# A hand-ordered Strassen kernel for AdaLN and FFN with LoRA experts: in the second pair VectorE makes two rests earlier and ranks experts later, and in the third pair GpSimd makes one rest ahead of a sum

## The reference

```python
y = einsum('bct,bcd->bdt', x, weights[condition])      # 64x64 per sample, chosen by index
result = einsum('bnd,od->bno', y, W_base) + b_base      # 1024 -> 1024
logits = einsum('bnd,ed->bne', y, W_gate)               # 8 experts
top_p, top_i = top_k(softmax(logits), 2)                # renormalised to sum 1
route_w = sum(one_hot(top_i, 8) * top_p[..., None], axis=-2)
hw = einsum('bnd,erd->bner', y, A) * route_w[..., None] # rank 16 each, 128 columns in all
delta = einsum('bner,eor->bno', hw, B)
out = x + result + delta                                # the scaling is 16/16 = 1
```

## Time and profile before

| | |
|---|---|
| median of 3 runs | 938.79 us |
| lowest and highest | 938.47 and 940.17 us |
| the profiled execution | 938.57 us, of which the span in the trace is 936.8 us |
| TensorE busy | 930.6 us, 99% of the span |
| TensorE weight loads | 877.6 us (beside the matmuls) |
| VectorE busy | 661.9 us, 71% |
| GpSimd busy | 529.3 us, 56% |
| ScalarE busy | 383.1 us, 41% |
| granted TensorE clock | 1.0 in the whole run's mean |

### The profile page before, as it was taken

How to read it: one execution, slowest core, us unless ns; L and a number is a source line. 1 busy time by engine, 2 the same in 40 slices (tenths; PEclk the granted TensorE clock), 3 DMA queues, 4 the chain that set the end, 5 groups by cost and what they waited for, 6 DMA issues and landing times.

```text
span 936.8 us, 17713 instructions
## 1 busy us (share of the span) xinstructions
PE 930.6 (99%) x5402; PEld 877.6 (94%) x5402; DVE 661.9 (71%) x2281; ACT 383.1 (41%) x817; POOL 529.3 (56%) x514
## 2 busy tenths in 40 slices
PE   9999999999999999999999999999999999999998
PEld 7989999999999999999999999999999999999998
DVE  5887667676677676676766767667767667676675
ACT  6743343443434434434334344343443443433432
POOL 2896555654556545566555565455664556655550
PEclk9999999999999999999999999999999999999999
DMA  9423333323333233232233332333323423223312
GB/s 316 170 72 131 124 112 112 107 83 123 121 103 123 78 112 134 91 132 90 101 123 112 112 103 87 123 121 103 123 82 108 134 95 129 90 100 123 112 68 90
DMA packets 41484, 107.13 MB, mean 114 GB/s; under 512 B 4481, under 2 KB 8706, under 8 KB 41474
## 3 DMA queue, kind: packets, MB, share of 16 engines
q1 hardware_dynamic: 40930, 106.47, 32.7%
q10 hardware_dynamic: 544, 0.54, 0.2%
HBM read 73.43 MB, written 33.55 MB: 114 GB/s over the span
## 4 chain that ended last, share of the span: by engine, by line
PE 98%; POOL 1%; DMA 0%; DVE 0%; issue 0%; ACT 0%; POOLq 0%; DVEq 0%
PE ps L875 56%; PE ps_r L875 19%; PE ps_out L893 11%; PE ps_out L903 9%; PE ps L934 1%; PE ps L945 1%; PE ps_r L934 1%; DMA r_raw<-in_w_t 0%; POOL s_sum L333 0%; POOL a_lo L322 0%; POOL raw L352 0%; PE ps_r L920 0%; PE ps L920 0%; POOL s_sum L339 0%; POOL s_sum L347 0%
## 5 line engine op out<-in xcount | busy, mean ns | idle before, releaser
L322 POOL TENSOR_TENSOR a_lo<-raw,a_hi 128x512 fp32r<-128x512 f32 x128 | 167.2, 1318 | 139.5 <-ACT a_hi L434 137.4
L678 DVE STREAM_TRANSPOSE ps_hwt<-hw 32x32 f32<-32x32 f32 x944 | 210.3, 223 | 29.6
L875 PE MATMUL ps<-w_hi,s_hi 128*128 128x448 f32 x492 | 180.7, 367 | 1.3 <-issue 0.8
L875 PE MATMUL ps<-w_lo,s_hi 128*128 128x448 f32 x492 | 178.5, 363 | 0.0
L875 PE MATMUL ps<-w_hi,s_lo 128*128 128x448 f32 x492 | 178.2, 362 | 0.0
L875 PE MATMUL ps_r<-r_lo,a_hi 128*128 128x264 f32 x488 | 139.0, 285 | 0.0
L875 PE MATMUL ps_r<-r_hi,a_hi 128*128 128x264 f32 x488 | 138.6, 284 | 0.0
L875 PE MATMUL ps_r<-r_hi,a_lo 128*128 128x264 f32 x488 | 138.5, 284 | 0.0
L875 PE MATMUL ps<-w_hi,a_hi 128*128 128x448 f32 x376 | 137.2, 365 | 0.0
L875 PE MATMUL ps<-w_hi,a_lo 128*128 128x448 f32 x376 | 136.9, 364 | 0.0
L875 PE MATMUL ps<-w_lo,a_hi 128*128 128x448 f32 x376 | 136.5, 363 | 0.0
(11 more groups left out here) (146 smaller groups left out, 1683.2 us busy)
## 6 DMA issues: line engine op xcount, KB each, us to landing
raw<-in_x_t SPq DMA_DIRECT2D x128, 256.0 KB, 2.6
o_sb<-in_x SPq DMA_DIRECT2D x64, 512.0 KB, 3.6
out_x<-o_sb SPq DMA_DIRECT2D x62, 512.0 KB, 2.7
w_sum<-in_w_t SPq DMA_DIRECT2D x6, 448.0 KB, 9.1
w_sum<-in_w_t SPq DMA_DIRECT2D x4, 224.0 KB, 5.5
r_raw<-in_w_t ACTq DMA_DIRECT2D x2, 264.0 KB, 4.6
r_raw<-in_w_t SPq DMA_DIRECT2D x2, 264.0 KB, 6.1
table_raw<-in_cond_w SPq DMA_DIRECT2D x2, 256.0 KB, 8.1
```

Source lines behind the costliest of these rows:

```text
L322: pool.tensor_tensor(a_lo[j][:], raw[j][:], as_f32(a_hi[j][:]), ALU.subtract).then_inc(s_a_lo[j], 1)
L678: dve.transpose(ps_hwt[c * TURN:(c + 1) * TURN, r * TURN:(r + 1) * TURN], hw[r * TURN:(r + 1) * TURN, c * TURN:(c + 1) * TURN]).then_inc(s ...
L875: mm = pe.matmul(bank[:, 0:w.shape[-1]], a[:, k, :], w[:, k, :], start=(opens and k == 0 and q == 0), stop=(closes and k == KH - 1 and q = ...
```

## The change

It moves instructions and adds or removes none.

- **DVE, second pair.** The gate of tile a (`rank_experts(1, 0)`, `weigh_experts(1, 0)`) stood ahead of T1's and T3's rests and now stands behind both and behind `u2`. `hwt_rest(2)` moves behind T4's rest. `u3` comes ahead of the sum that adds P3, and the three outputs of tile a move behind the sums of P5 and P4.
- **PE, second pair.** `turn_hw(2)` moves from the half of P6 to the half of P7. Lora L and R of tile a move from ahead of P4 to behind it.
- **ACT, second pair.** T3's top and three tops of the third pair's input come ahead of the gate's exponential. The seeds and S3's top move back.
- **POOL, third pair's preparation.** S2's rest stands ahead of S3's sum.

SP's list is the same.

```diff
@@ POOL, first()
                 sum_s4(2)
+                s_rest(2, 2, s2[:], s2_hi, s2_lo)
                 sum_s3(2)
-                s_rest(2, 2, s2[:], s2_hi, s2_lo)
                 s_rest(2, 3, s3[:], s3_hi, s3_lo)
@@ ACT, first()
                 z_top(1, R, ps_5[:, 0:width[R]])
-                exps(2)
                 t_top(3, T3)
-                pe_hwt_top(3)
                 a_top(2, A11)
                 act.wait_ge(s_p[3], 2)
                 a_top(2, A12)
                 a_top(2, A21)
+                exps(2)
+                pe_hwt_top(3)
                 added_top(1, 0, Q, ps_r[:, 0:NS])
-                seed(1, 1, L)
                 added_top(1, 1, Q)
                 sum_top(2, 2, s2[:], s2_hi)
                 added_top(1, 1, L)
-                sum_top(2, 3, s3[:], s3_hi)
+                seed(1, 1, L)
                 seed(1, 1, R)
                 sum_top(2, 1, s1[:], s1_hi)
                 act.wait_ge(s_p[4], 2)
                 a_top(2, A22)
                 seed(1, 1, Q)
+                sum_top(2, 3, s3[:], s3_hi)
@@ DVE, first()
                 z_rest(1, 0, R, ps_r[:, 0:width[R]])
-                rank_experts(1, 0)
-                weigh_experts(1, 0)
                 z_rest(1, 1, R, ps_5[:, 0:width[R]])
                 t_rest(1, T1)
-                hwt_rest(2)
                 t_rest(3, T3)
                 dve.wait_ge(s_p1_out, 1)
                 dve.wait_ge(s_p[6], 2)
                 add(ps_6, p1, u2).then_inc(s_u2, 1)
+                rank_experts(1, 0)
+                weigh_experts(1, 0)
                 t_rest(4, NT4)
+                hwt_rest(2)
+                dve.wait_ge(s_p[7], 2)
+                add(ps_6, p1, u3).then_inc(s_u3, 1)
                 dve.wait_ge(s_p[3], 2)
                 dve.wait_ge(s_u2, 1)
                 add(ps_1, u2, u2).then_inc(s_p3_in, 1)
-                dve.wait_ge(s_p[7], 2)
-                add(ps_6, p1, u3).then_inc(s_u3, 1)
@@ PE, first()
-                strassen(ps_6, s2_hi, s2_lo, T2, True, lambda: turn_hw(2)).then_inc(s_p[6], 1)
+                strassen(ps_6, s2_hi, s2_lo, T2, True).then_inc(s_p[6], 1)
...
-                strassen(ps_6, s3_hi, s3_lo, T3, False).then_inc(s_p[7], 1)
+                strassen(ps_6, s3_hi, s3_lo, T3, False, lambda: turn_hw(2)).then_inc(s_p[7], 1)
                 mix_chunk(1, 0, R)
+                pe.wait_ge(s_t_lo[4], 1)
+                pe.wait_ge(s_u3, 1)
+                strassen(ps_6, a_hi[A22], a_lo[A22], NT4, False).then_inc(s_p[4], 1)
                 pe.wait_ge(s_hwt_lo, 3)
                 lora(0, L)
                 lora(0, R)
-                pe.wait_ge(s_t_lo[4], 1)
-                pe.wait_ge(s_u3, 1)
-                strassen(ps_6, a_hi[A22], a_lo[A22], NT4, False).then_inc(s_p[4], 1)
```

More of the change, by code:

```diff
@@ L794, in first @@
                 add(ps_5, u2, ps_r[:, 0:NS]).then_inc(s_z_sum[0, Q], 1)
-                output(1, 0, L)
                 added_rest(1, 0, Q, ps_r[:, 0:NS])
@@ L798, in first @@
                 add(ps_5, u3, u3).then_inc(s_z_sum[1, Q], 1)
-                output(1, 0, R)
                 added_rest(1, 1, Q)
@@ L802, in first @@
                 add(ps_6, p1, added[1, L]).then_inc(s_z_sum[1, L], 1)
+                output(1, 0, L)
                 added_rest(1, 1, L)
+                output(1, 0, R)
                 output(1, 0, Q)
```

## The result

| | before | after |
|---|---|---|
| median | 938.70 us (13 runs) | 940.46 us (13 runs) |
| lowest and highest | 938.46 and 940.28 | 939.90 and 943.23 |
| the profiled execution | 938.57 (span 936.8) | 941.5 (span 939.8) |

The ratio is 1.0023, with a 95% interval of 1.0015 to 1.0031: the change makes the kernel **slower by 0.2%**, just over the bound up to which I had called a difference none. The ratio is worked out from all executions; the two medians alone are 1.76 us, or 0.19%, apart.

What follows compares the result with a forecast made beforehand. PE, busy for 99% of the span, was taken to bound the kernel, so only its waits count. New waits of 2.69 less old ones of 2.32 gave +0.37 us and 939.1 us, with a range of 937.9 to 940.7.

Steps and rivals of the forecast that it cites:

- What bounds the kernel: PE busy for 99% of the span; the change moves only its waits in that stretch, 2.3 us at most to win.
- my second case: Rival of two port turns lost: the sum of S2 goes ahead of T4's rest, P4 at 63.08; +1.45, 940.2 us, chance 0.30.
- The exclusive port: A DVE operation with both inputs in SBUF and a POOL operation don't run together; the later waits for the whole earlier one.
- T4's rest, issued "at 59.10": On DVE ahead of P4: ends at 61.12 if the port is free, P4 starts at 62.00 and waits 1.00.
- the case of T3 first: T3's rest gets the port before S3's rest: P7 at 57.07, P4 at 61.83, +0.2 us; one turn lost has chance 0.45.
- The order of T1's and T3's rests: On DVE ahead of P7: S3's rest on POOL goes between them, P7 starts at 57.62, 1.17 us late.
- the sum of the new waits, 2.69: New waits of PE at P5, P7, the turn and P4 with restarts, against 2.32 of old ones: +0.37 us.
- within 0.2%: Whole kernel: a difference below 0.2% (1.9 us), not to be told from no change; chance 0.85.
- the floor at P4: With lora L and R moved, nothing hides `u3`: 0.60 us of wait and 0.09 restart even with DVE free.
- it takes away the wait of 0.69: S2's rest 1.29 us earlier on POOL removes the third pair's P6 wait of 0.69 and its 0.09 restart.
- A third turn lost: Rival: after the sum of S2, T4's rest also waits for the rest of A11 on POOL; +2.75, 941.6 us, chance 0.07.
- No turn lost: Rival: T3's and T4's rests get the port ahead of POOL, P4 at 60.91; -0.7, 938.1 us, chance 0.12.

Runs made afterwards that it cites:

- e3: The changed kernel with POOL waiting for T4's rest before it makes the sum of S2; 939.18 us, ratio 1.0004 against the kernel before.
- e10: The changed kernel with POOL waiting for T3's rest before it makes S3's rest, nothing else ordered; 939.04 us, ratio 1.0004 against the kernel before.
- e5: The changed kernel with POOL waiting for T3's rest before S3's rest and for T4's rest before the sums of S1 and S2; 937.92 us, ratio 0.9993.
- e8: The changed kernel with the gate's move undone on DVE, ACT and PE, the rest of the change kept; 938.87 us, ratio 1.0005.
- e2: The changed kernel with the POOL part undone, S3's sum ahead of S2's rest again; 941.59 us, ratio 1.0026.
- e1: The kernel before with the POOL part alone, S2's rest ahead of S3's sum; 938.93 us, ratio 1.0002.
- e6: The kernel before with S2's rest ahead of S3's sum and, on ACT, S3's top behind the seed of Q; 937.81 us, ratio 0.9991.
- e4: The changed kernel with 12 matmuls of zeros on PE ahead of the wait for P4; 940.29 us, ratio 1.0016.

## Why the prediction was wrong

**What bounds the kernel: right.** Only PE's waits moved, and at full clock the trace after can be laid beside my second case row by row: P5 54.02 forecast and 53.94 found, T3's rest 3.1 us and 3.11, P7 57.62 and 57.55, the turn 59.24 and 59.18, P4 63.08 and 62.98, the sum +1.45 and +1.4. (Up to 0.1 us of each difference in the starts comes from ahead of the change: T2's rest, which wasn't moved, already starts at 47.78 and not 47.88.) The forecast of that case, 940.2, is 0.2 from 940.0, the middle of the seven executions at full clock. That it is also only 0.3 from the measured median of 940.46 is luck: 940.46 is the slowest of these seven, and with one more execution at the lower clock the median would have been 941.5. The exclusive port, which I had read from the stretched durations in the earlier trace rows, carried all of this.

**The step that failed is that T4's rest, issued "at 59.10", "ends at 61.12 if the port is free".** My own count had the sum of S2 on POOL at 59.02, 0.08 us ahead, and I took the other side for the forecast and gave it 0.45 together with the case of T3 first. It was worth 1.0 us (e3). The count was right: found are 58.94 and 59.04, a margin of 0.10. The Trainium skill's rule in SBUF - State Buffer ("Who interferes with whom"), that the first to issue holds the pair of ports for its whole instruction, gave 940.2, and e10 shows it to hold at 0.03 us. I had written that none of the rows has so small a margin. That was a wrong reading: in the earlier trace rows T1's rest is issued at 53.20 and POOL's cast at 53.23, and the rest took its 2.02 us while the cast took 2.13 (0.29 when it is free, as at 57.20 in the trace of after). The earlier one had the port there too, at 0.03 us. I had set against the rule the warning of the Trainium skill's Perfetto Trace Analysis ("GPSIMD Engine Instruction") that GpSimd's spans are unreliable, and my own doubt about sums of a dozen terms. Neither was a reason to take the other side: both engines hung on the same event, the end of T3's rest, so most of the terms were common and their errors cancelled. The doubt was a reason for even odds at most.

**The order of T1's and T3's rests was right.** S3's rest went in between, as it had been waiting. The way in which it cost was right too: e5 and e10 take it away, and P7 comes 0.3 earlier (57.23 in e5; the wait ahead of it is 0.7 and not 1.1), with a further 0.3 at the turn.

**The second step that failed: the sum of the new waits, 2.69, has no term for the clock.** I listed 2.7 us of new waits and restarts within 8 us and, in the second case, 3.8, but no term for what PE's clock does after them; the trace of before has no such place in its middle, and I took the full clock for granted. The fall of the clock adds 1.6 us to six of 13 executions, 0.7 on average, and so lifts the ratio from what the waits give (1.4 in 936.8, 0.15%) to 0.23%, over the bound. That is why "within 0.2%" with 0.85 was too sure, even had I named the second case.

**The lora's move and the floor at P4: right in size.** 0.60 was forecast for an otherwise free DVE; e8 shows 0.61 (0.73 less 0.12). **The POOL part: right for the changed kernel, as far as its runs tell** (e2). But "it takes away the wait of 0.69" would have been wrong by itself: in the order of before the wait only moves on to the mix of b's Q (e1). It was the move of S3's top on ACT, which I had not weighed, that makes the gain real (e6).

**The rivals.** A third turn lost (941.6) didn't happen: T4's rest had its turn next after the sum of S2, and the rest of A11, issued at 60.18, waited for it. No turn lost was priced at 938.1 and, when e5 enforced it, measured at 937.92.

## What to carry to other kernels

Where an operation of DVE with two inputs in SBUF and POOL's work stand close, put their issue times on one line and let the earlier one have the port, even at a margin of some hundredths; then settle the order with a wait instead of leaving it to chance, since one wait added to POOL gained 1.0 us here and two gained 2.1. When the sum of a change contains several waits of TensorE close together, price the clock as well: with 2.1 us idle ahead of P4 it fell in half of the executions and cost as much as the waits. And when an operation moves back on one engine, look at what stands behind its consumers in the other engines' queues: the gain of S2's rest was lost to a seed in that way.

## What the hardware did that I had not expected

The granted clock fell to 0.50 while PE was busy, after the idle time and not in it: the first steps of P4 (up to 64.07) were still at the full rate. It did so in some executions of one and the same program and not in others (6 of 13, 5 of 8, 7 of 11), at a price of 1.6 us each time. A microsecond and a half of matmuls of zeros in the wait was enough to keep it (e4). Why one execution is hit and another not is open; no run here was made to tell. The Trainium skill, TensorE: Matmul & The Clock Gate (Part 1, "What's actually happening"), says of the warm-up at a kernel's start that one kernel gets through a different number of matmuls before the switch from run to run. Here it is a fall in the middle of a kernel, and it too comes in some runs and not in others.
